# A general softmax path moved behind the end of each engine's program

## The reference

```python
h = _layernorm(x) * (1 + ca) + sa
q = h.reshape(B, T, 16, 8).transpose(0, 2, 1, 3)        # keys and values are q too
scores = einsum('bhqd,bhkd->bhqk', q, q) * 8 ** -0.5
attn = softmax(scores * palace_mask, axis=-1)            # 1 where t % 8 agree, else sigmoid(w)
x = x + ga * einsum('bhqk,bhkd->bhqd', attn, q)
h = _layernorm(x) * (1 + cb) + sb
x = x + gb * (shared_mlp(h) + top3_of_15_experts(h))
```

## Time and profile before

| | |
|---|---|
| median of 3 runs | 373.64 us (372.37 to 373.94) |
| the profiled execution | 373.84 us |
| its span, first to last instruction | 372.1 us |
| PE busy | 338.4 us (91%) |
| ACT busy | 288.0 us (77%) |
| DVE busy | 185.9 us (50%) |
| POOL busy | 33.0 us (9%) |

### The profile page before, as it was taken

The page is one execution under the profiler, slowest core; times in us unless marked ns, Lnnn a source line. Parts: engine busy times, 40 slices in busy tenths (PEclk is TensorE's granted clock), DMA queues, the critical chain, the costliest instruction groups (busy, mean ns, idle before and its releaser), DMA issues.

```text
span 372.1 us, 6245 instructions
## 1 busy us (share of the span) xinstructions
PE 338.4 (91%) x2365; PEld 153.6 (41%) x2365; DVE 185.9 (50%) x499; ACT 288.0 (77%) x265; POOL 33.0 (9%) x47
## 2 busy tenths in 40 slices
PE   3849899999999998999989899999989999999995
PEld 2532322222323322333222333223458577777773
DVE  6993113533442310425513525101489988797884
ACT  3647999999999999999999999999525344444442
POOL 4891000521000000100000100000010000000000
PEclk9999999999999999999999999999999999999998
DMA  7785899024000399200000000930200089460000
GB/s 218 252 304 175 290 348 295 4 82 174 2 0 5 131 322 384 99 2 3 2 2 0 2 0 7 409 128 2 113 1 2 0 318 405 157 202 26 28 2 29
DMA packets 23631, 45.78 MB, mean 123 GB/s; under 512 B 2254, under 2 KB 10096, under 8 KB 22060
## 3 DMA queue, kind: packets, MB, share of 16 engines
q1 hardware_dynamic: 23160, 44.92, 34.2%
q10 hardware_dynamic: 436, 0.39, 0.3%
HBM read 31.56 MB, written 13.75 MB: 122 GB/s over the span
## 4 chain that ended last, share of the span: by engine, by line
PE 61%; DVE 13%; issue 11%; ACT 10%; DMA 2%; POOL 1%; ACTq 0%; DVEq 0%
PE acc L1302 23%; PE slot L1190 13%; ACT prob L661 10%; PE spare L1142 4%; PE slot L1332 3%; PE slot L1334 3%; PE slot L1333 3%; PE slot L1357 3%; DVE oT L970 3%; PE slot L1355 2%; PE slot L1354 2%; PE slot L1349 2%; DVE prob L1098 2%; DVE glo L1106 2%; DMA wcol<-attn_inter_palace_weight 2%
## 5 line engine op out<-in xcount | busy, mean ns | idle before, releaser
L661 ACT ACTIVATE prob<-slot 128x1536 f32<-128x1536 f32 x171 | 234.7, 1469 | 11.2 <-PE slot L1190 10.7
L1302 PE MATMUL acc<-prob,val 128*9 128x512 f32 x1024 | 135.1, 600 | 5.2 <-DVE oT L970 4.7
L1190 PE MATMUL slot<-QQ,KK 32*128 32x512 f32 (+1 forms) x768 | 92.9, 409 | 10.5 <-issue 5.1
L1190 PEld LDWEIGHTS slot<-QQ,KK 32*128 32x128 f32 x768 | 43.9, 187 | 129.4 <-ACT prob L661 87.2
L690 ACT ACTIVATE ghi<-prob 128x512 fp32r<-128x512 f32 x52 | 32.9, 632 | 50.6 <-DVE prob L1098 49.9
L970 DVE COPY oT<-acc 128x512 f32<-128x512 f32 x16 | 11.1, 691 | 84.5 <-PE acc L1302 84.5
L1106 DVE SCALAR_TENSOR_TENSOR glo<-prob,ghi 128x512 fp32r<-128x512 f32 x52 | 35.5, 682 | 0.4
L1098 DVE SCALAR_TENSOR_TENSOR prob<-slot,bcol,KK 128x512 f32<-128x512 f32 x37 | 27.6, 749 | 6.8 <-PE slot L1334 6.5
L1332 PE MATMUL slot<-h2hi,w1h 128*128 128x512 f32 x64 | 30.6, 478 | 0.0
L1302 PEld LDWEIGHTS acc<-prob,val 128*9 128x9 f32 x1024 | 15.5, 88 | 34.2 <-issue 29.2
L547 POOL TENSOR_TENSOR rstd<-rstd,power 128x4 f32<-128x4 f32 (+1 forms) x6 | 7.4, 1229 | 233.7 <-DVE rstd L764 233.7
(11 more groups left out here) (179 smaller groups left out, 247.7 us busy)
## 6 DMA issues: line engine op xcount, KB each, us to landing
KK<-cw_d SPq DMA_DIRECT2D x7, 1024.0 KB, 8.5
rows<-cw_d SPq DMA_DIRECT2D x5, 1024.0 KB, 5.1
KK<-kd SPq DMA_DIRECT2D x14, 256.0 KB, 5.2
QQ<-qd SPq DMA_DIRECT2D x14, 256.0 KB, 5.5
KK<-kw SPq DMA_DIRECT2D x14, 256.0 KB, 6.4
KK<-cw_d SPq DMA_DIRECT2D x3, 768.0 KB, 9.0
rows<-in_L_ffn_eW SPq DMA_DIRECT2D x2, 960.0 KB, 7.4
kd<-w2h SPq DMA_DIRECT2D x2, 512.0 KB, 5.3
```

The lines of the kernel that those rows point to most:

```text
L661: nc.scalar.activation(ring[:, at:at + n * CH], slot[u % 2][:, 0:n * CH], ACT.Exp, scale=SCALE).then_inc(exp_done, 1)
L1190: return mm(dst, KK[n][r, s, c * M:(c + 1) * M], QQ[n][r, lo:hi], start=True, stop=True, tile_position=(32 * q, 0))
L1302: last = mm(acc[32 * q:32 * q + HD + 1], val[:, b, n, c, q, :], prob[:, (G * cl + q) % RING], start=c == 0, stop=c == C - 1, tile_position ...
```

## The change

On PE, DVE and SP the body of the general path moves from behind the branch to behind the last instruction of the engine's usual program. The branch is the same comparison with the general path as its other target; the general path ends with a jump back to the usual code, and the usual code ends with a jump over the general path to the common end. The three hint instructions go. No other operation is added, removed or reordered on the usual path.

```diff
+        def branch_to_general(eng, name):
+
+            wanted = exact_wanted(eng)
+            eng.br_lt(wanted, 1, on_true=f"{name}_main", on_false=f"{name}_general")
+            before = nc.cur_bb
+            nc.switch_bb(f"{name}_main")
+            return before
+
         @contextmanager
-        def exact_part(eng, kind, wanted, ahead, name):
-
-            eng.br_lt(wanted, 1, on_true=f"{name}_after", on_false=f"{name}_body").branch_hint(ahead)
-            outer = nc.cur_bb
-            with nc.bb(f"{name}_body", parent=outer, valid_engines=[kind]):
+        def general_path(eng, kind, name, before):
+
+            eng.br(f"{name}_end")
+            with nc.bb(f"{name}_general", parent=before, valid_engines=[kind]):
                 yield
-                eng.br(f"{name}_after")
-            nc.switch_bb(f"{name}_after")
+                eng.br(f"{name}_main")
+            nc.switch_bb(f"{name}_end")
...
-            sp_ahead = sp.mark_branch_hint_location()
-            exact = exact_wanted(sp)
-            with exact_part(sp, mybir.EngineType.SP, exact, sp_ahead, "exact_sp"):
-                sp.wait_ge(spart_ok, 1)
...
+            before = branch_to_general(sp, "sp")
             sp.sem_inc(go, 1)
...
             sp.wait_ge(out_wr, 16 * STAGES)
+
+            with general_path(sp, mybir.EngineType.SP, "sp", before):
+                sp.wait_ge(spart_ok, 1)
...
             feature_rows(("zT", 0, 0, 0))
-            dve_ahead = dve.mark_branch_hint_location()
...
-            exact = exact_wanted(dve)
-            with exact_part(dve, mybir.EngineType.DVE, exact, dve_ahead, "exact_dve"):
+            before = branch_to_general(dve, "dve")
```

More of the change, by code:

```diff
@@ L517, in _ @@
             sp.wait_ge(out_wr, 16 * STAGES)
+            with general_path(sp, mybir.EngineType.SP, "sp", before):
+                sp.wait_ge(spart_ok, 1)
+                for k in range(2):
+                    sp.dma_start(shift_d[k].rearrange("(b h) (c m) -> b (h c) m", b=B, c=C).rearrange("b q m -> q b m"),
+                                 as_f32(spart[:, k]).rearrange("q (b m) -> q b m", b=B)).then_inc(shift_wr, 16)
+                sp.dma_start(xz[:, 1], x[1].rearrange("(m c) d -> m c d", c=C)).then_inc(ex_ld, 16)
+                sp.wait_ge(shift_wr, 32)
+                sp.wait_ge(planes_wr, 16 * 3 * B)
+                for k in range(2):
+                    for b in range(B):
+                        sp.dma_start(qd[b].rearrange("(h d) w t -> d w h t", d=HD)[k, WAYS - 1],
+                                     shift_d[k][H * b:H * (b + 1)]).then_inc(ex_ld, 16)
+                    for q in range(G):
+                        at = 32 * q + WAYS * k + WAYS - 1
+                        sp.dma_start(as_f32(QQ[0][at:at + 1, :]), shift_d[k][q:q + 1]).then_inc(ex_ld, 16)
+                sp.wait_ge(ex_ld, 16 * (1 + 2 * B + 2 * G))
         @block.gpsimd
@@ L1134, in _, with chain @@
             take_back(("back", LAST, 0, 0))
+            with general_path(dve, mybir.EngineType.DVE, "dve", before):
+                told = [0]
+                def chain(ins):
+                    told[0] += 1
+                    ins.then_inc(ex_seq, 1)
+                    dve.wait_ge(ex_seq, told[0])
+                dve.sem_inc(ex_max, 2)
+                dve.wait_ge(z_ok, 1)
+                dve.wait_ge(zp_ok, 1)
+                dve.wait_ge(vrow_ok, 1)
+                for k in range(2):
+                    for n in range(1, NG):
+                        spread_weights(v.tensor_copy, k, n).then_inc(ex_wmr, 1)
+                dve.wait_ge(ex_cols, 1)
+                ex_mod = spare[:, 0:2 * NG * B].rearrange("p (k n b) -> p k n b", k=2, n=NG)
+                chain(affine(aP[:], bP[:], ex_mod[:, SA], ex_mod[:, CA]))
+                chain(v.memset(zr_scan, 0.0))
+                for b in range(B):
+                    if b:
+                        dve.wait_ge(ld_x[2], 16)
+                        moments(z1, 0, C, chain)
+                        scan_root(C, chain)
+                        chain(normalised(z1, z1, 0, C))
+                    for n in range(NG):
+                        for p in range(PARTS):
+                            last = v.tensor_copy(replica(zr_scan, p), group_of(b, n))
+                        last.then_inc(ex_z, 1)
+                        for half in range(HALVES):
+                            k = HALVES * (NG * b + n) + half
+                            dve.wait_ge(ex_zT, k + 1)
+                            build_half(b, n, spare[:], m_plain, chain, chain, half_cols(half), 1).then_inc(ex_built, 1)
+                            dve.wait_ge(ex_built, k + 1)
+                        for u in range(G * C):
+                            k = G * C * (NG * b + n) + u
+                            dve.wait_ge(ex_mm, k + 1)
+                            v.reduce_max(shift[:, b].rearrange("p h c -> p (h c)")[:, G * C * n + u:G * C * n + u + 1],
+                                         slot[k % 2][:, 0:T], AX.X, negate=True).then_inc(ex_max, 1)
+                dve.wait_ge(shiftT_mm, 1)
+                sT = spare[:, 0:B * M]
+                chain(v.tensor_copy(spart[:, 0], sT))
+                v.tensor_tensor(spart[:, 1], sT, as_f32(spart[:, 0]), ALU.subtract).then_inc(spart_ok, 1)
+                dve.wait_ge(go, 1)
@@ L1178, in _ @@
             pe.wait_ge(gate_ok, 2)
-            pe_ahead = pe.mark_branch_hint_location()
             for b in range(B):
@@ L1191, in score @@
                           tile_position=(32 * q, 0))
[L1193 to L1227, removed]
+            before = branch_to_general(pe, "pe")
             def side(use):
@@ L1368, in _ @@
             side(("back", LAST, 0, 0))
+            with general_path(pe, mybir.EngineType.PE, "pe", before):
+                pe.wait_ge(taken, USE["zT", 0, 0, 0])
+                pe.wait_ge(t1_ok, 1)
+                pe.wait_ge(built, 1)
+                pe.wait_ge(ex_wmr, 2 * (NG - 1))
+                for k in range(2):
+                    for n in range(NG):
+                        at = (NG * k + n) * B
+                        last = spread_columns(spare[:, at:at + B], k, n)
+                last.then_inc(ex_cols, 1)
+                for b in range(B):
+                    for n in range(NG):
+                        pe.wait_ge(ex_z, NG * b + n + 1)
+                        for half in range(HALVES):
+                            k = HALVES * (NG * b + n) + half
+                            if k:
+                                pe.wait_ge(ex_built, k)
+                            half_turn(spare[:], zr_scan, half).then_inc(ex_zT, 1)
+                        pe.wait_ge(ex_built, HALVES * (NG * b + n + 1))
+                        for q in range(G):
+                            for c in range(C):
+                                k = G * C * (NG * b + n) + q * C + c
+                                pe.wait_ge(ex_max, k + 1)
+                                dst = slot[k % 2]
+                                for half in range(HALVES):
+                                    score(dst[:, half_cols(half)], 1, q, half * CH, half * CH + CH, c, 0)
+                                score(dst[:, c * M:(c + 1) * M], 1, q, c * M, (c + 1) * M, c, 1).then_inc(ex_mm, 1)
+                pe.wait_ge(ex_max, 2 + B * H * C)
+                for b in range(B):
+                    last = nc.tensor.transpose(spare[:, b * M:(b + 1) * M], shift[:, b].rearrange("p h c -> p (h c)"),
+                                               ident[:])
+                last.then_inc(shiftT_mm, 1)
+                pe.wait_ge(spart_ok, 1)
+                pe.wait_ge(go, 1)
 _INS = ["L0_attn_x", "L0_attn_inter_palace_weight", "L0_ffn_router_W", "L0_ffn_router_b", "L0_ffn_sW1",
```

## The result

The changed kernel takes **370.20 us** (median of 4 runs, 369.92 to 370.51); the kernel before, run beside it, 373.28 (4 runs, 372.37 to 373.94). The ratio is 0.9903, with a 95% interval of 0.9881 to 0.9925: 3.1 us, 0.8%, faster. Forecast were 370.5 us and 3.1 us gained.

A forecast was written before the change was run, and what follows sets the result against it. PE, 91% busy, stood 5.08 us at its taken branch while code was fetched; DVE stalled likewise; then ACT's exponentials set the pace. −4.3 at the start + 1.2 at the end = −3.1: 370.5 us, range 368.9 to 372.8 (about 0.83).

The forecast's parts named there:

- PE's branch: At 17.5 us on PE: falls from 5.22 us to about 0.07, so the first scores start 5.0 us earlier.
- Rival 3: The stalls belong to testing the register, not the jump; start stays, end costs 1.2 us: 374.8 us; chance 0.06.
- What catches up: Start, producers not moving with PE: POOL's values no loss, unit 5 leaves 4.6 us, unit 16 leaves 4.3 us.
- the 4.3 us: Net gain at the start after units 5 and 16 wait for operands; bounds 3.5 and 4.8 us.
- the DVE half of the reasoning: Behind DVE's branch: resumes 3.4 us earlier, so unit 16's last load lands at 43.1 us instead of 46.2.
- no later load is as tight as unit 16's: Between start and end: an assumption by which the start's shift is carried through unchanged.
- Rival 2: Start catches up less: half-1 writes collide with loads, or PE stays longer at the lower clock; 372.5 us; chance 0.11.
- PE's clock: Start: the step from 1.2 to 2.4 GHz comes 5.0 us earlier, at 27.3 us; no term.
- The end: New jumps: PE's 5.2 us to 373.0, DVE's 3.5 to 372.7, SP stays at 371.8; costs 1.2 us, bounds 0 and 1.5.
- Rival 1: The end is free, its jumps fetched in time or made cheaper by the missing wait: 369.3 us; chance 0.11.
- Rival 4: At the end PE pays 5.2 us twice, ending 6.4 us behind SP: 375.7 us; chance 0.06.
- Hints: The removed hints are one instruction each and nothing waits for them: 0.

The follow-up runs named there:

- e4b_after_again: The changed kernel run again without any edit, beside the kernel without the general path: 370.38 us (369.97 to 370.99).
- e2_pe_moved: Against the kernel before, only PE's general path moved; DVE and SP keep the old form, hints included: 373.18 us, ratio 0.9983.
- e7_quiet_dma: The kernel before, with SP waiting for the first unit's scores before it writes the planes of `qd`: 373.87 us in one run.
- e6: The changed kernel plus a hint for PE's and DVE's jump at the end, six jobs ahead: 370.23 us (369.65 to 371.03).
- e3: Against the kernel before, only DVE's general path moved; the other engines keep the old form, hints included: 373.91 us, ratio 1.001.
- e11: The changed kernel with hints for the end jumps, DVE's 22 jobs ahead and PE's 3.9 us ahead: 374.75 us in one run, total not read.
- e1_no_hints: The kernel before with its three hints taken out and nothing moved: 373.93 us, ratio 1.0002.
- e4: The changed kernel without the general path (no branch, body or end jump; flag still read): 369.33 us, ratio 0.9897.
- e5: The kernel without the general path run again, unedited, beside the changed kernel: 369.19 us (369.14 to 369.63).

## Why the prediction was right, and where it was not

**PE's branch: right.** 5.22 to 0.07 was forecast, 86 ns measured, scores 5.1 us earlier once the late transposes are set off. Rival 3, the branch dear in itself, is gone: the same comparison on the same engine costs 86 ns when its target follows, and 5195 without the hint when it doesn't.

**What catches up: right in mechanism, and the 4.3 us partly luck.** Unit 5 waited for DVE's keys (1.24 us at 28.04). ACT's shift there is 4.28 us; forecast for that place were 4.6, which is what comes out once the 0.27 us are set off by which this execution was late before its branch, and what the second profile has (4.56 in e4b_after_again). The last load for unit 16 landed at 43.12 us, forecast 43.1, but it took next to nothing from ACT where 0.3 was forecast; in e4b_after_again it landed at 43.69 and took 0.9. At ACT's end the shift is 4.2 and 3.6 us in the two profiles, between the lower bound of 3.5 and the forecast of 4.3. e2_pe_moved shows that the DVE half of the reasoning was needed: without it ACT's lead at the end is 2.3 us in the profile, and by the medians the gain is 0.8 us and not distinct from none. The sentence that no later load is as tight as unit 16's did not hold in e2, where a later one costs PE 0.83 us. Rival 2 did not come.

**PE's clock: no term, as said, but the step came sooner.** PE's six scores take 0.90 us at 22.54, which is the lower of its two levels (1.2 GHz), and 0.56 from 25.26 on, the upper (2.4). I had put the step at 27.3. It bought nothing, because unit 5 waits for DVE.

**The end: a cost of the right sign, by another path and smaller in the trace.** The step that failed is "PE's jump is as long as the one removed: 5.2 us, so 373.0". It took 3.3 us (3.6 and 3.9 in e2 and e4b). e7_quiet_dma shows that 1.5 of the 5.2 was queueing behind data that the end doesn't have. So PE drains 1.0 us before SP (0.2 and 0.5 in e2 and e4b), and e6 shows that this jump is covered. The second step that failed is that SP "stays at 371.8", with the last store untouched. What costs is a resource I had not counted: DVE's fetch runs beside the last store, on the same DMA engines, and the store takes 2.8 us instead of 2.0 with nothing of DVE's beside it, or 2.5 as before. DVE's own jump took 2.9 us where 3.5 were forecast, and ends with the store. Behind ACT's end that is 0.8 us against a kernel without jumps, and 0.4 against the kernel before. Forecast were 1.2. Rival 1, a free end, is wrong in form, since PE's jump took 3.3 us and the store is longer; its 0 is nearer to the 0.4 than the forecast's 1.2. Rival 4 did not come, since neither engine paid twice.

**Hints: 0 in the sum, but not in its parts.** The time less the span is 1.7 to 1.9 us in every run of the kernels that carry PE's hint (before, e3, e6 to e11) and 2.1 to 2.3 in every run of those that don't (after, e1, e2, e4, e5). So the changed kernel's span fell by 3.9 us, but its profiled time by 3.44. Whether the hint saves this or the span only begins at another point, the runs don't tell. Against it stands that the kernels without PE's hint have a quicker end: e1_no_hints loses 0.4 us outside the span and wins 0.5 behind ACT's end (4.48 against 4.97), and its median is 0.1 from that of the kernel before.

**The sum.** −4.2 at ACT's end, +0.4 behind it, +0.4 outside the span make −3.4 for the profiled pair, and −3.1 by the medians. Forecast was −4.3 + 1.2. Put by causes, the jumps cost 0.8 at the end and the missing hints −0.5 behind ACT's end and +0.4 outside the span, which is −4.2 + 0.8 − 0.1, nearly the same. So the 1.2 was too large by 0.4, and the 4.3 stands against 4.2 in one profile of the changed kernel and 3.6 in the other; the hit within 0.3 us is partly luck. The bounds were also added up wrongly: gains of 3.5 to 4.8 and losses of 0 to 1.5 give 368.8 to 371.6 us, not 369.3 to 371.8. The measured median lies in both.

## What to carry to other kernels

In this kernel a taken jump over hundreds of operations cost PE 3.3 to 5.2 us and DVE 2.9 to 4.6 each time that its code was not fetched ahead, while the condition alone cost under 0.1 us. Look for "issue" time right behind a branch line, and let the usual path fall through, or put the hint far ahead and check that the branch line becomes short. If the price moves to the end, it is hidden only if some wait covers the jump and the fetch does not share the DMA engines with the last store. When two engines stall side by side, freeing one alone may bring nothing (DVE's here) or keep only a part (PE's).

## What the runs showed of the hardware that was not expected

- Code fetches and data share the DMA engines in both directions: a data transfer makes a jump 1.5 us longer (5221 against 3684 ns), and the fetches for the jumps make a 256 KB store 0.8 us longer (2.0 against 2.8 us), most of it DVE's.
- A hint that is served shortens the jump (5221 to 406 ns), but not every hint is served: at the start not with 4.0 us of lead on PE and 7.6 on DVE, at the end with 3.9 us on PE and not with 13.6 on DVE.
- DVE's branch line never shows its jump: 51 to 90 ns are recorded, and the 3 us stand as "issue" or as a late drain behind it. PE's line shows the whole of it.
- The kernel before scatters from 371.3 to 376.7 us over its 25 runs beside the first four kernels; the changed one stays within 369.9 to 371.0 in 8. No run was made on why.
